# Scores of plain attentions: two tiles of 64 rows at a time, four neighbouring heads per tile, one spread of the keys for eight heads

## The chip, the core and the metric

One Trainium2 chip, one of its cores. The metric is the device time of one execution in microseconds; a smaller number is faster. The kernel before takes 2011.68 us, the median of 3 runs (2011.1 to 2012.37).

## What is computed

Four transformer layers, one after the other, on 16 sequences of 128 tokens with 256 features. Layer 0 has a small attention among the 16 heads of a token. Layer 1 has two attentions with quantised scores and weights. Layers 2 and 3 have two ordinary ("plain") attentions each, the ones that the change touches; all use 16 heads of 16 features. In the reference a plain attention is, cut to what matters (layer 2's form; layer 3 is the same with a mask of minus infinity in its second attention and none in its first):

```python
qh = split(q @ wq + bq)
kh = split(k @ wk + bk)
vh = split(v @ wv + bv)
logits = jnp.einsum('bhqd,bhkd->bhqk', qh, kh) / jnp.sqrt(jnp.float32(depth))
if mask is not None:
    logits = logits + mask * -1000000000.0
attn = jax.nn.softmax(logits, axis=-1)
out = jnp.einsum('bhqk,bhkd->bhqd', attn, vh)
```

Around each attention stand an output projection, a residual sum, a layer norm and, once per layer, a feed-forward net of width 1024. Everything is float32 here.

## The kernel before

The 16 sequences are worked in 4 groups; a group has two streams (`st` 0 and 1) of two sequences (G = 2). Each engine has its instructions written out in one fixed order. `together` lays the 13 steps of one stream's attention and the "pieces" of the other stream (projections, norm, transposes, feed-forward, the next keys) beside each other: on each engine step 0, its pieces, step 1, its pieces, and so on. On PE the pieces come after the step of their number; on ACT, DVE and POOL most come one step later (LATE = 1). Nothing is reordered at run time, so an instruction that waits holds all that stand behind it on its engine.

One attention of a stream has U = 8 units u: 2 sequences j times 4 sets of four heads. For a plain attention a unit goes through these stages:

- **Spread of the keys** (`spread`, line 1300, POOL). KT holds 128 rows, that is 8 heads of 16 rows. For unit u the tile KB gets four copies of the keys side by side, each with the rows of one head kept and all others zero (times own_head), so that one matmul gives the scores of four heads. Even units take heads 0, 2, 4, 6 of the eight, odd units 1, 3, 5, 7. There are 4 such tiles (NK), and the spreads run up to 3 units ahead (KEYS_AHEAD).
- **Scores** (`scores`, line 806, PE). One matmul over 128 rows and 512 columns into PSUM bank u % 2. It waits until the bank was read: by the mask addition of unit u - 2 where there is a mask, otherwise by the exponentials of unit u - 2. A float32 matmul stands in the trace as two instructions.
- **Mask and row maximum** (`shift`, lines 1183 and 1187, DVE). With a mask, line 1183 adds it and writes to the SBUF tile prob, which frees the bank; line 1187 takes the maxima.
- **Exponentials** (line 990, ACT), four per unit; from prob, or from the bank without a mask.
- **Turn** (`turn`, line 816, PE), four transposes, two steps later, and their copy to SBUF (line 976, ACT).
- **Values** (`values_pair`, line 850, PE) for two units together: products with V and with ones, in column tiles of 32. Then DVE divides (`outputs`, lines 1217 and 1219).

The quantised attentions of layer 1 already spread keys in bf16 for eight heads at once and use halves of 64 rows (lines 1295 and 804), one unit per step.

The plain attentions of layers 2 and 3 are 32: 4 groups, 2 layers, 2 streams, 2 attentions. In the order of time, the first attention of stream 0 and of stream 1 have the feed-forward's last product or its neighbours beside them, the second of stream 0 has the short pieces, the second of stream 1 has the next layer norm, projections and feed-forward.

## Time and profile before

| what | value |
|---|---|
| median of 3 runs | 2011.68 us |
| the profiled execution's own time | 2007.97 us |
| its span in the trace | 2006.2 us |
| PE busy | 1808.6 us (90%) |
| DVE busy | 1237.6 us (62%) |
| ACT busy | 1074.7 us (54%) |
| POOL busy | 905.3 us (45%) |

Times in the views count from the span's start. PE is the matmul engine, PEld its loading of weights, which lies beside the matmuls; DVE, ACT and POOL are VectorE, ScalarE and GpSimd. A matmul's duration in a row contains its latency, so matmuls that follow each other overlap in the rows; what one costs in a stream is the distance between starts. "Idle before" tells how long an engine stood still and what ended that. The chain of waits is followed back from the last instruction.

### The profile page before, as it was taken

The numbers are of one execution on the slowest core, as the hardware profiler recorded it, in microseconds if no ns is written. First come the engines' busy times: TensorE is split into PE (matmuls) and PEld (weight loads), VectorE is DVE, ScalarE is ACT, GpSimd is POOL, SyncE is SP. The second block draws the span as 40 slices with busy tenths as digits, with TensorE's granted clock in tenths as the row PEclk, the third lists the DMA queues.
The fourth block names the chain that finished last, engine by engine and source line by source line (L and its number), as shares of the span: only waits on it lengthen the run. The fifth ranks groups of instructions, "written<-read, shape, count | busy, mean of one in ns | idle before, by whom it ended". The sixth has DMA issues, their size and how long they took to land.

```text
span 2006.2 us, 34807 instructions
## 1 busy us (share of the span) xinstructions
PE 1808.6 (90%) x12481; PEld 1344.1 (67%) x12481; DVE 1237.6 (62%) x2220; ACT 1074.7 (54%) x3142; POOL 905.3 (45%) x1209
## 2 busy tenths in 40 slices
PE   4998988789799889889999999999999999999997
PEld 4887876466566656657667677676676676766766
DVE  5899995744654464463575665865746647365471
ACT  2232225665575475565575564655645656565662
POOL 4466554654463363363254443644444333333340
PEclk8999998788878878879999999999999999999999
DMA  7200000002000000000002000000000000000000
GB/s 226 92 11 6 11 6 6 1 7 90 1 6 6 1 6 6 0 6 7 1 7 90 1 7 6 7 7 1 7 6 2 12 1 7 22 7 1 12 1 11
DMA packets 31073, 35.66 MB, mean 18 GB/s; under 512 B 3164, under 2 KB 29752, under 8 KB 30520
## 3 DMA queue, kind: packets, MB, share of 16 engines
q1 hardware_dynamic: 30904, 33.44, 5.2%
q8 instruction: 102, 1.67, 0.3%
q14 instruction: 67, 0.55, 0.1%
HBM read 31.34 MB, written 2.10 MB: 17 GB/s over the span
## 4 chain that ended last, share of the span: by engine, by line
PE 61%; DVE 17%; ACT 10%; issue 6%; POOL 2%; SPq 2%; DMA 1%; DVEq 0%; POOLq 0%; ACTq 0%
PE ps L594 33%; PE ps L806 6%; PE ps L744 6%; PE ps L816 5%; PE ps L850 4%; ACT work L983 3%; ACT work L990 3%; DVE work L1183 3%; DVE xn L1037 2%; PE ps L607 2%; DVE rowmax L1187 2%; PE ps L831 2%; ACT hT L899 1%; PE ps L766 1%; POOL work L1376 1%
## 5 line engine op out<-in xcount | busy, mean ns | idle before, releaser
L594 PE MATMUL ps<-hT,w_slot 128*128 128x256 f32 x1696 | 410.1, 396 | 17.1 <-ACT hT L899 16.1
L1300 POOL TENSOR_TENSOR work<-KT,own_head 128x512 f32<-128x512 f32 x256 | 262.4, 1046 | 285.4 <-PE ps L806 179.9
L594 PEld LDWEIGHTS ps<-hT,w_slot 128*128 128x128 f32 x1696 | 323.5, 196 | 77.2 <-ACT hT L899 21.7
L990 ACT ACTIVATE work<-work,rowmax 128x128 f32<-128x128 f32 x768 | 244.9, 391 | 167.8 <-DVE rowmax L1187 167.0
L816 PEld LDWEIGHTS ps<-ident,work 128*128 128x128 f32 x1536 | 200.1, 153 | 170.0 <-issue 90.4
L983 ACT ACTIVATE work<-ps,rowmax,score_scale 128x128 f32<-128x128 f32 x512 | 229.3, 484 | 118.7 <-DVE rowmax L1191 118.3
L816 PE MATMUL ps<-ident,work 128*128 128x128 f32 x1536 | 266.4, 302 | 17.9 <-ACT work L990 17.0
L806 PE MATMUL ps<-work,QT 128*128 128x512 f32 x512 | 266.4, 605 | 10.0 <-POOL work L1300 4.9
L1376 POOL TENSOR_SCALAR work<-work,winv 128x128 f32<-128x128 f32 x512 | 185.0, 382 | 167.7 <-DVE winv L1203 165.3
L1217 DVE RECIPROCAL O<-ps 128x128 f32<-128x128 f32 x128 | 122.3, 955 | 174.6 <-PE ps L850 173.9
L976 ACT ACTIVATE work<-ps 128x512 f32<-128x512 f32 x256 | 150.7, 596 | 91.4 <-PE ps L816 91.2
L1316 POOL TENSOR_SCALAR vareps<-meanvar 128x2 f32<-128x2 f32 x88 | 19.3, 220 | 383.0 <-DVE meanvar L1030 379.9
L1059 DVE TENSOR_TENSOR x_all<-ps,x_all 128x512 f32<-128x512 f32 x72 | 49.7, 690 | 154.1 <-PE ps L594 89.0
L947 ACT ACTIVATE hid<-ps,vcols 128x256 f32<-128x256 f32 x192 | 80.7, 472 | 106.6 <-PE ps L594 106.5
L1037 DVE TENSOR_SCALAR xn<-x_all,meanvar,rstd 128x256 f32<-128x256 f32 x176 | 128.4, 769 | 13.0 <-POOL rstd L1318 12.7
L1187 DVE TENSOR_REDUCE rowmax<-work 128x4 f32<-128x512 f32 x192 | 131.8, 686 | 6.6
L1295 POOL TENSOR_TENSOR work<-QKb,own_quad 128x512 bf16<-128x512 bf16 x64 | 70.2, 1116 | 130.5 <-issue 125.0
L594 PE MATMUL ps<-w_slot,OT 128*128 128x256 f32 x448 | 119.6, 414 | 6.4 <-ACT OT L931 4.8
L804 PE MATMUL ps<-work,QKb 64*128 64x512 bf16 x128 | 62.8, 501 | 66.7 <-ACT work L983 47.7
L983 ACT ACTIVATION_READ_ACCUMULATOR work<-ps,rowmax,score_scale 128x1 f32 x512 | 118.2, 231 | 0.0
L744 PE MATMUL ps<-w_slot,hid 128*128 128x256 f32 x512 | 116.5, 381 | 1.6 <-ACT hid L947 0.9
L974 ACT ACTIVATE work<-ps,top 128x512 bf16<-128x512 f32 x128 | 90.5, 707 | 50.3 <-PE ps L816 49.3
(131 smaller groups left out, 3170.3 us busy)
## 6 DMA issues: line engine op xcount, KB each, us to landing
ctx_in<-in_ctx SPq DMA_DIRECT2D x32, 256.0 KB, 2.7
w_slot<-in_L_xattn_W SPq DMA_DIRECT2D x2, 1024.0 KB, 6.2
w_slot<-in_L_xattn_ff_w SPq DMA_DIRECT2D x1, 2048.0 KB, 11.5
w_slot<-in_L_xattn_ffn_w SPq DMA_DIRECT2D x2, 1024.0 KB, 9.8
w_slot<-in_L_xattn_w SPq DMA_DIRECT2D x2, 1024.0 KB, 10.0
out<-x_all SPq DMA_DIRECT2D x8, 256.0 KB, 2.1
x_all<-in_x SPq DMA_DIRECT2D x1, 1536.0 KB, 11.4
pad<-in_mask_Bx1x1xS_fk SPq DMA_DIRECT2D x1, 1024.0 KB, 7.6
```

Of the source, the lines that this page charges most:

```text
L594: mm = pe.matmul(dst, lhsT(k), rhs(k), start=(k == 0 and not onto), stop=(k == chunks - 1 and not more))
L744: mm = pe.matmul(one[:, j * D:(j + 1) * D], hid[:, k, tok(j)], w[arg["w2"]][:, k, :], start=(k == 0), stop=(k == FC - 1))
L806: pe.matmul(bank(u % 2), QT[st][:, m, tok(j)], KB[u % NK], start=True, stop=True).then_inc(s["scores_ps"], 1)
L816: mm = pe.transpose(bank(2 + u % 2)[:, tok(h)], prob[u % (NP if quant else NPF)][:, tok(h)], ident[:, :])
L976: act.activation(PTF[u % 4], bank(2 + u % 2), ACT.Copy).then_inc(s["PT_ready"], 1)
L983: ex = act.activation(prob[i % NP][:, tok(h)], bank(i % 2)[:, tok(h)], ACT.Exp, bias=shifts[:, at:at + 1], scale=score_scale[:, arg["quant ...
L990: ex = act.activation(prob[i % NPF][:, tok(h)], src[:, tok(h)], ACT.Exp, bias=shifts[:, at:at + 1])
L1037: dve.tensor_scalar(xn[st][:, j, :].unsqueeze(1), x_of(g, st, j), meanvar[st][:, j, 0:1], rstd[st][:, j:j + 1], ALU.subtract, ALU.mult).th ...
L1187: dve.tensor_reduce(shift_u, sc, AX.X, ALU.max, negate=True).then_inc(s["shift_ready"], 1)
L1217: dve.reciprocal(oinv[st][quarter], bank(4 + m)[:, sums_at:sums_at + S]).then_inc(s["oinv_ready"], 1)
L1300: pool.tensor_tensor(KB[u % NK].rearrange("p (h k) -> p h k", h=HU), keys, own_head[:, e:HC:2].unsqueeze(2).broadcast_to([P, HU, S]), ALU. ...
L1376: w = pool.tensor_scalar(prob[u % NP][:, tok(h)], prob[u % NP][:, tok(h)], winv[:, u // 2 % 2, at:at + 1], MAGIC, ALU.mult, ALU.add)
```

## The change

A plain attention now makes its scores for two units at once. At each even step PE issues the scores of units u and u + 1: rows 0 to 63 of QT and of one spread tile give the four lower heads into bank 0, rows 64 to 127 the four upper heads into bank 1. It is four matmuls of 64 rows and 256 columns: left half of the columns for both row halves, then right half. They signal once, by 2, at the end. The odd steps have no scores.

The wait ahead of them is for what has freed both banks: the mask addition of unit u - 1, or the exponentials of unit u - 1. The wait for V, which stood before the scores of unit 1, is now at step 1.

The spread is done once for two units, with the table own_four (row r belongs to head r // 16, folded to four columns), so 4 instead of 8 spreads per attention, of the same form. The 4 tiles hold the 8 units of an attention, and a spread waits only for the scores that used its tile in the attention before. The values take their columns from the turned tiles in the new order of heads; their number and form stay.

```diff
--- before.py
+++ after.py
@@ -276,6 +276,7 @@
         ident = sb("ident", [P, P])
         own_head = sb("own_head", [P, HC])
         own_quad = sb("own_quad", [P, HU], BF16)
+        own_four = sb("own_four", [P, HU])
         ones_pair = sb("ones_pair", [P, 4, DH])
         vcols = sb("vcols", [P, P])
         vcols_q = sb("vcols_q", [P, len(Q_BIASES) * C])
@@ -791,19 +792,24 @@
                         att = use("att", layer, g, n["att"])
                         pe.wait_ge(q["q_ready"], C * (att + 1))
                         pe.wait_ge(q["k_ready"], C * (att + 1))
-                    if u == 1:
-                        pe.wait_ge(q["v_ready"], G * (use("att", layer, g, n["att"]) + 1))
                     pe.wait_ge(s["KB_ready"], U * ap + u + 1)
-
-                    if u >= 2 and "mask" in arg:
-                        pe.wait_ge(s["masked"], U * masked_phase(layer, g, mix, st) + u - 1)
-                    else:
+                    if quant:
+
                         pe.wait_ge(s["exp_ready"], U * ap + u - 1)
-                    if quant:
                         half = slice(u % 2 * (P // 2), (u % 2 + 1) * (P // 2))
                         pe.matmul(bank(u % 2), QTb[st][half, m, tok(j)], KBb[u // 2][half, :], start=True, stop=True).then_inc(s["scores_ps"], 1)
+                        return
+
+                    if u and "mask" in arg:
+                        pe.wait_ge(s["masked"], U * masked_phase(layer, g, mix, st) + u)
                     else:
-                        pe.matmul(bank(u % 2), QT[st][:, m, tok(j)], KB[u % NK], start=True, stop=True).then_inc(s["scores_ps"], 1)
+                        pe.wait_ge(s["exp_ready"], U * ap + u)
+                    for part in range(2):
+                        cols = slice(part * US // 2, (part + 1) * US // 2)
+                        for e in range(2):
+                            half = slice(e * (P // 2), (e + 1) * (P // 2))
+                            mm = pe.matmul(bank(e)[:, cols], QT[st][half, m, tok(j)], KB[u // 2][half, cols], start=True, stop=True)
+                    mm.then_inc(s["scores_ps"], 2)
 
                 def turn(u):
                     if quant:
@@ -847,12 +853,14 @@
                         for e in range(2):
                             for h in range(HU):
                                 own = ones_pair[:, 2 * e:2 * e + 2, :] if summed else V[st][:, j, m * HU + h, 2 * e:2 * e + 2, :]
-                                mm = pe.matmul(bank(4 + m)[h * 32:(h + 1) * 32, cols], own, PTF[(u + e) % 4][:, tok(h)],
+                                mm = pe.matmul(bank(4 + m)[h * 32:(h + 1) * 32, cols], own, PTF[(u + h // 2) % 4][:, tok(2 * (h % 2) + e)],
                                                start=(e == 0), stop=(e == 1))
                     mm.then_inc(s["o_ps"], 2)
 
                 def step(i):
-                    if i < U:
+                    if i == 1:
+                        pe.wait_ge(q["v_ready"], G * (use("att", layer, g, n["att"]) + 1))
+                    if i < U and (quant or i % 2 == 0):
                         scores(i)
                     if 0 <= i - lag < U:
                         turn(i - lag)
@@ -1281,7 +1289,7 @@
                 q, mix, quant = c[st], n["att"], "quant" in arg
                 ap = phase("att", layer, g, mix, st)
 
-                j, m, e = u // UJ, u % UJ // 2, u % 2
+                j, m = u // UJ, u % UJ // 2
                 if u == 0 and layer == 1 and mix == 0 and st == 0 and g == 0:
 
                     pool.wait_ge(s["o_ready"], G * phase("mix", layer, g, mix, st))
@@ -1295,11 +1303,10 @@
                     pool.tensor_tensor(KBb[u // 2].rearrange("p (h k) -> p h k", h=HU), keys,
                                        own_quad[:, :].unsqueeze(2).broadcast_to([P, HU, S]), ALU.mult).then_inc(s["KB_ready"], 2)
                     return
-                pool.wait_ge(s["scores_ps"], U * ap + u + 1 - NK)
+                pool.wait_ge(s["scores_ps"], U * ap + u - 6)
                 keys = KT[st][:, m, tok(j)].unsqueeze(1).broadcast_to([P, HU, S])
-                pool.tensor_tensor(KB[u % NK].rearrange("p (h k) -> p h k", h=HU), keys,
-                                   own_head[:, e:HC:2].unsqueeze(2).broadcast_to([P, HU, S]), ALU.mult)\
-                    .then_inc(s["KB_ready"], 1)
+                pool.tensor_tensor(KB[u // 2].rearrange("p (h k) -> p h k", h=HU), keys,
+                                   own_four[:, :].unsqueeze(2).broadcast_to([P, HU, S]), ALU.mult).then_inc(s["KB_ready"], 2)
 
             def emit_piece(layer, g, st, ahead=False, shift={}):
                 q = c[st]
@@ -1308,7 +1315,7 @@
                 def emit(piece, arg, n):
                     if piece == "keys":
                         for u in range(KEYS_AHEAD):
-                            if "quant" not in arg or u % 2 == 0:
+                            if u % 2 == 0:
                                 spread(layer, g, st, arg, n, u)
                     elif piece == "norm":
                         k = due("norm", layer, g, n["norm"])
@@ -1380,7 +1387,7 @@
                 def step(i):
 
                     u = i + KEYS_AHEAD - 1
-                    if i > 0 and u < U and (not quant or u % 2 == 0):
+                    if i > 0 and u < U and u % 2 == 0:
                         spread(layer, g, st, arg, n, u)
                     if quant and 0 <= i - SUM_LAG - 1 < U:
                         weigh(i - SUM_LAG - 1)
@@ -1401,6 +1408,7 @@
                                pattern=[[DH, HC]], channel_multiplier=-1).then_inc(s["own_ready"], 1)
             pool.wait_ge(s["own_ready"], 1)
             pool.tensor_tensor(own_quad[:, :], own_head[:, 0:HU], own_head[:, HU:HC], ALU.add)
+            pool.tensor_tensor(own_four[:, :], own_head[:, 0:HU], own_head[:, HU:HC], ALU.add)
             pool.memset(neg_half[:, :], -0.5)
             pool.memset(top[:, :], MAGIC + 255.0)
             pool.memset(below[:, :], -255.0)
```

PE, from the third scores on, in the first attention of layer 3 (no mask), stream 1, as it was. `work,QT` are scores, `ident,work` the transposes of a unit, `work,V` and `work,ones_pair` the values of two units, `ident,xn` the other stream's transposes.

```order
L806 MATMUL ps<-work,QT 128x512
L816 MATMUL ps<-ident,work 128x128 x4
L806 MATMUL ps<-work,QT 128x512
L816 MATMUL ps<-ident,work 128x128 x4
L806 MATMUL ps<-work,QT 128x512
L816 MATMUL ps<-ident,work 128x128 x4
L850 MATMUL ps<-work,V 32x128 x8
L850 MATMUL ps<-work,ones_pair 32x128 x8
L806 MATMUL ps<-work,QT 128x512
L816 MATMUL ps<-ident,work 128x128 x4
L806 MATMUL ps<-work,QT 128x512
```

The same place on PE, from the second scores on, as it is now:

```order
L811 MATMUL ps<-work,QT 128x256 x4
L822 MATMUL ps<-ident,work 128x128 x8
L811 MATMUL ps<-work,QT 128x256 x4
L822 MATMUL ps<-ident,work 128x128 x4
L856 MATMUL ps<-work,V 32x128 x8
L856 MATMUL ps<-work,ones_pair 32x128 x8
L822 MATMUL ps<-ident,work 128x128 x4
L811 MATMUL ps<-work,QT 128x256 x4
L822 MATMUL ps<-ident,work 128x128 x4
L856 MATMUL ps<-work,V 32x128 x8
```

Before, a transpose of a finished unit stood between the scores of any two units. Now the second scores row carries units 4 and 5, and the transposes of unit 2 and all values of units 0 and 1 stand behind it.

POOL, between two attentions of layer 2: `KT,own_head` and `KT,own_four` are spreads, `vareps` and `rstd` the other stream's norm, the rest its x; as it was.

```order
L1300 TENSOR_TENSOR work<-KT,own_head 128x512 x6
L1316 TENSOR_SCALAR vareps<-meanvar 128x2
L1318 TENSOR_TENSOR rstd<-vareps,neg_half 128x2
L1300 TENSOR_TENSOR work<-KT,own_head 128x512 x2
L1325 TENSOR_TENSOR x_all<-xn,rows 128x512
L1328 TENSOR_TENSOR x_all<-x_all,rows 128x512
L1338 TENSOR_TENSOR x_all<-x_all,rows 128x512
```

The same place on POOL as it is now:

```order
L1308 TENSOR_TENSOR work<-KT,own_four 128x512 x3
L1323 TENSOR_SCALAR vareps<-meanvar 128x2
L1325 TENSOR_TENSOR rstd<-vareps,neg_half 128x2
L1308 TENSOR_TENSOR work<-KT,own_four 128x512
L1332 TENSOR_TENSOR x_all<-xn,rows 128x512
L1335 TENSOR_TENSOR x_all<-x_all,rows 128x512
L1345 TENSOR_TENSOR x_all<-x_all,rows 128x512
```

Three spreads in place of six lie together ahead of the norm, and one in place of two behind it.

## Rows read from the trace of the kernel before

**Rows 1.** The page, busy time of each engine (us, share of the span, instructions).

```profile
PE 1808.6 (90%) x12481; PEld 1344.1 (67%) x12481; DVE 1237.6 (62%) x2220; ACT 1074.7 (54%) x3142; POOL 905.3 (45%) x1209
```

**Rows 2.** The page, the chain that ended last, by engine and by line.

```profile
PE 61%; DVE 17%; ACT 10%; issue 6%; POOL 2%; SPq 2%; DMA 1%; DVEq 0%; POOLq 0%; ACTq 0%
PE ps L594 33%; PE ps L806 6%; PE ps L744 6%; PE ps L816 5%; PE ps L850 4%; ACT work L983 3%; ACT work L990 3%; DVE work L1183 3%; DVE xn L1037 2%; PE ps L607 2%; DVE rowmax L1187 2%; PE ps L831 2%; ACT hT L899 1%; PE ps L766 1%; POOL work L1376 1%
```

**Rows 3.** Windows; columns: length, busy PE, PEld, DVE, ACT, POOL, clock, DMA, GB/s.

```profile
1072.59:1111.98 39.39, 37.85 (x285) 28.95 (x284) 22.34 (x40) 21.34 (x58) 17.70 (x18) 1.00 0.34 114
1624.63:1655.89 31.26, 29.98 (x245) 21.95 (x244) 13.30 (x24) 17.55 (x49) 10.27 (x11) 1.00 0.00 1
1655.89:1681.71 25.82, 23.74 (x213) 15.69 (x212) 18.82 (x33) 16.46 (x46) 9.40 (x11) 1.00 0.01 2
950.00:1960.00 1010.00, 959.20 (x7815) 698.55 (x7814) 613.55 (x1100) 599.31 (x1642) 419.28 (x441) 1.00 0.03 10
```

**Rows 4.** Groups by line: busy us, mean ns of one; idle before, who ended it.

```profile
L806 PE MATMUL ps<-work,QT 128*128 128x512 f32 x512 | 266.4, 605 | 10.0 <-POOL work L1300 4.9 <-DVE V L1080 2.4 <-ACT work L990 2.3
...
L1300 POOL TENSOR_TENSOR work<-KT,own_head 128x512 f32<-128x512 f32 x256 | 262.4, 1046 | 285.4 <-PE ps L806 179.9 <-ACT KT L911 105.1
...
L804 PE MATMUL ps<-work,QKb 64*128 64x512 bf16 x128 | 62.8, 501 | 66.7 <-ACT work L983 47.7 <-DVE V L1011 10.9 <-DVE QKb L1011 5.8
...
L806 PEld LDWEIGHTS ps<-work,QT 128*128 128x128 f32 x512 | 85.6, 190 | 38.7 <-issue 20.8 <-DVE V L1080 10.6 <-POOL work L1300 2.0
```

**Rows 5.** Chain of waits, 1586.89 to 1716.68 us; start, us, what.

```profile
1651.39 1.73 PE ps L594 x8
```

**Rows 6.** Timeline of PE, masked attention that begins at 1072.59.

```profile
1072.59 1.02 PE L806 MATMUL ps<-work,QT 128*128 128x512 f32 x2
...
1077.24 1.02 PE L806 MATMUL ps<-work,QT 128*128 128x512 f32 x2
...
1094.00 1.02 PE L806 MATMUL ps<-work,QT 128*128 128x512 f32 x2
...
1097.19 1.99 PE L594 MATMUL ps<-w_slot,O 128*128 128x256 f32 x8 [0.73 <-ACT KT L911]
```

**Rows 7.** Timeline of DVE, same attention.

```profile
1093.71 0.68 DVE L1183 TENSOR_TENSOR work<-ps,look 128x512 f32<-128x512 f32 x1
```

**Rows 8.** Timeline of PE, unmasked attention that begins at 1624.63.

```profile
1638.65 1.10 PE L806 MATMUL ps<-work,QT 128*128 128x512 f32 x2 [0.57 <-ACT work L990]
...
1642.53 1.02 PE L806 MATMUL ps<-work,QT 128*128 128x512 f32 x2
1643.39 0.60 PE L816 MATMUL ps<-ident,work 128*128 128x128 f32 x4
1643.92 0.65 PE L850 MATMUL ps<-work,V 128*32 128x128 f32 x16
...
1645.42 1.02 PE L806 MATMUL ps<-work,QT 128*128 128x512 f32 x2
```

**Rows 9.** Timeline of DVE, same attention.

```profile
1641.26 0.96 DVE L1217 RECIPROCAL O<-ps 128x128 f32<-128x128 f32 x1 [0.79 <-PE ps L850]
```

**Rows 10.** Instructions of line 1037 (durations in ns, min/median/max).

```profile
L1037 DVE TENSOR_SCALAR xn<-x_all,meanvar,rstd x176: 395/412/4620, 58.7 to 1982.4; 128x256 f32<-128x256 f32 x176
```

**Rows 11.** Timeline of DVE around 1178 us.

```profile
1178.60 2.07 DVE L1037 TENSOR_SCALAR xn<-x_all,meanvar,rstd 128x256 f32<-128x256 f32 x2
```

**Rows 12.** Timeline of POOL, same stretch.

```profile
1178.19 1.28 POOL L1338 TENSOR_TENSOR x_all<-x_all,rows 128x512 f32<-128x512 f32 x1
1179.43 1.09 POOL L1300 TENSOR_TENSOR work<-KT,own_head 128x512 f32<-128x512 f32 x1
```

**Rows 13.** Timeline of PE in a quantised attention, 64-row score matmul and its successor.

```profile
312.36 0.39 PE L804 MATMUL ps<-work,QKb 64*128 64x512 bf16 x1 [0.74 <-DVE V L1011]
312.67 1.99 PE L594 MATMUL ps<-w_slot,OT 128*128 128x256 f32 x8
```

**Rows 14.** Windows in the same quantised attention (columns as in rows 3).

```profile
320.00:325.00 5.00, 4.46 (x22) 2.35 (x21) 4.08 (x13) 4.93 (x18) 4.74 (x12) 0.50 0.01 3
```

## The prediction

> **What bounds the kernel now.** I read the busy shares first: PE is busy for 90% of the span, DVE for 62%, ACT 54%, POOL 45% [rows 1]. The chain of waits says the same with less certainty: 61% of it is PE, 17% DVE, 10% ACT, and the plain score matmuls (line 806) are 6% of it, about 120 us [rows 2]. The windows then say where: the 32 plain attentions fill 950 to 1960 us, with PE busy for 959 of 1010 us and the granted clock at its upper level of 2.4 GHz throughout [rows 3]. That looks like a pure PE bound, and it is not quite one. In the masked attention without large pieces beside it (1655.89 to 1681.71) DVE is busy for 18.8 of 25.8 us, and a unit must pass score, mask, maximum, exponential, transpose, copy and values in turn. PE's order is fixed, so what counts is where PE's saving meets a wait. Layers 0 and 1, which end before that window, are untouched.
>
> **Part 1: the score matmuls themselves.** A float32 matmul of 256 columns costs 1.73 / 8 = 0.216 us per instruction, two instructions each [rows 5]. The score matmul of one unit has 512 columns and two instructions, so 4 x 0.216 = 0.86 us in a stream; this is also the distance from 1642.53 to 1643.39 [rows 8]. Two units: 1.73 us. The new block of four 64-row matmuls of 256 columns has eight instructions of 0.216 us. If the upper and lower rows run beside each other it takes 0.86 us, if not, 1.73 us. To this comes the change of shape of the array: full transposes started at 1643.39 and the column-tiled values at 1643.92, 0.53 us for four transposes that stream in 0.44, so 0.09 us for entering another tiling [rows 8]. For leaving the 64-row form, the bf16 score at 312.36 was followed 0.31 us later [rows 13], against 512 columns / 2.4 GHz = 0.21 us: 0.10 us. I take 0.86 + 0.09 + 0.10 and add 0.10 us for weights, since the block loads eight times where two units loaded four times: **1.15 us per block**, bounds 0.86 and 1.9 us. I stand near the lower end because the column-tiled values, also float32, do overlap: from 1643.92 to 1645.42 PE starts 32 of them and four transposes [rows 8], where 32 x 0.108 us one by one would be 3.5 us. PE's work shrinks by 128 x (1.73 - 1.15) = 74 us. The Trainium skill ("TensorEngine Tiling (Array Packing)", Key Properties) says that changing the tiling mode drains the engine; the 0.09 us agrees. The skill ("TensorE: Matmul & The Clock Gate", Measured speedup vs the span model) gives 3.07 for four row tiles; an estimate from that efficiency, 0.77, is a block of 1.12 us before the switches, and by it the gain below would be about 7 us smaller.
>
> **Part 2: the coarser wait.** Before, the scores of u waited for the bank of u - 2. Now the block of u and u + 1 waits for u - 1, and the transposes of u - 2 and the values of u - 4 and u - 3 are queued behind it. DVE and ACT wait for these. I went through the eight kinds of attention with PE's new order and the old durations; two show the pattern.
> *Masked, with the feed-forward beside it (from 1072.59).* Three score matmuls, of units 1, 3 and 5, go ahead of the one at 1094.00 [rows 6], 2.6 us. But the last block needs the mask addition of unit 5, which began at 1093.71 and took 0.68 us [rows 7]. DVE is early only by the one matmul (0.86) that stood before its first block. So the block starts at 1093.71 + 0.68 + 0.15 - 0.86 = 1093.7 and some 2 us of the saving become waiting. The next piece waited for KT, which ACT writes behind the exponentials of unit 5 (1097.19 [rows 6]); it comes about 1 us sooner, and with the score of unit 7 gone from behind it the attention ends 1.4 us sooner.
> *Unmasked, stream 1 (from 1624.63).* Block (4, 5) waits for the exponentials of unit 3, some 0.75 us later than the old wait for unit 2 at 1638.65 [rows 8]. Then come: block and transposes 1.3, values 1.1, the reciprocal (0.96 [rows 9]) and its product 0.3, the norm 0.7, the maximum 0.7, the exponentials of unit 5 1.2: block (6, 7) starts 6.3 us after block (4, 5), at 1645.7, where unit 6 started at 1642.53 and unit 7 at 1645.42. The transposes and values that used to stand between 6 and 7 now come after. This one ends **2.1 us later** even with a perfect block.
> With a block of 0.86 us, layer 2 gains 1.4, 1.0, 0.6 and 0.9 us in its four attentions per group, and layer 3 gains 0.3, -2.1, 0.25 and 0.4. Four groups: 4 x (3.9 - 1.15) = **11 us gained**. With 1.15 us instead, the excess of 0.3 us shows once or twice per attention, mostly in the tail where PE is never idle: 8 kinds x 0.45 x 4 = 14, say **15 us lost**.
>
> **Part 3: POOL.** 256 spreads of 1.05 us become 128, so 134 us less [rows 4]. POOL is at 45%, and its spreads mostly stood waiting for the scores (179.9 us of idle before them), so by itself this is worth nothing; no POOL wait becomes longer, since a spread now needs only scores of the attention before. But DVE's normalisation (line 1037) takes 0.41 us at the median and up to 4.6 [rows 10]; at 1178.60 two of them took 2.07 us [rows 11], while POOL ran x and then a spread from 1179.43 [rows 12]. It seems to be held by the POOL instruction that runs. One of the two spreads behind the norm disappears. I count 0.7 us in each kind with a spread between, 0.4 to 0.5 in the others, none in one: 3.9 us per group, and all of it is ahead of the block (6, 7): 4 x 3.9 = **16 us gained**, bounds 0 and 20.
>
> **Sum.** 11 - 15 + 16 = 12 us. The profiled execution took 2007.97 us (span 2006.2), so 1996; against the median of 2011.68, which is 3.7 us above it, **2000 us**. With the block at 0.86 us it is 1985, and without the POOL term 2016. About 4 us (0.2%) is what a measurement can tell from no change.
>
> **The rivals.**
> *A, the halves don't overlap (0.13).* The trace has no float32 row tiles side by side. The weights of a score matmul load in 190 ns [rows 4]; two such loads lie in one pass of 216 ns only if loads overlap as well. The skill ("TensorE: Matmul & The Clock Gate", LDWEIGHTS) says that a load's time goes with columns, not rows, which is against this change. A block of 1.9 us, 0.75 more than taken, costs 4 x 8 x 0.45 / 0.3 x 0.75 = 36 us: 2036. It decides from a block of about 1.4 us on.
> *B, slower by the coarser wait (0.17).* If DVE and ACT have less slack than I read, each masked attention loses its 1 us gain and 0.5 more, at the last block: 24 x 1.5 = 36 us worse than the sum, 2036; with half of it, 2018. For it speaks the DVE-bound stretch of 1655.89 [rows 3]; against it that most blocks there are issued while DVE does other pieces.
> *C, much faster (0.15).* The chain gives line 806 6% of the span [rows 2]; if PE truly bounds, 74 us less work shortens the span by some 45: 1967. Against it: the waits in part 2.
> *D, the clock falls (0.06).* In the quantised attentions PE did little for some microseconds and the clock granted was 0.50, that is 1.2 GHz [rows 14]. The plain attentions now give PE longer waits. If 1.5 us of PE work in each of 16 short attentions takes twice as long, that is 24 us: 2024.
> *E, nothing to see (0.10).* Parts 2 and 3 cancel: 2012.
>
> **How the numbers follow.** The forecast, 1985 to 2006, has 0.39. Faster by over 0.2%: 0.39 + C 0.15 = 0.54. Within 0.2%: most of E and a little of B, 0.13. Slower: A, D, the rest of B and E, 0.33. The range leaves out what lies beyond C and A: 1967 to 2036.
>
> **What would show it.** Right: the distance from a block's start to the next instruction is 1.1 to 1.2 us; PE idles before line 811 for exponentials or masked tiles, in all by tens of us; PE busy falls by 60 to 80 us while the span falls by 12; the first unmasked attention of stream 1 is 2 to 3 us longer and those of layer 2 are 1 us shorter; two normalisations take 0.8 to 1.4 us instead of 2. Wrong: a distance of 1.7 us or more (A), the masked attentions of layer 2 longer (B), all eight kinds 1.5 us shorter (C), a granted clock below 1.00 between 950 and 1960 us (D).

## The result, and the profile after

The changed kernel takes 2027.86 us (median of 4 runs, 2026.9 to 2029.31) beside 2011.39 us of the kernel before: ratio 1.0089, 95% interval 1.0075 to 1.0103. It is slower by 0.9%, where 2000 us was forecast. The value lies in the range, the sign is wrong. The profiled execution took 2029.31 us with a span of 2027.6 us.

The page's busy times and its groups on the lines that changed (line 806 is now 811, line 1300 is 1308; columns as in [rows 1] and [rows 4]):

```profile
PE 1761.1 (87%) x12993; PEld 1359.9 (67%) x12993; DVE 1211.4 (60%) x2220; ACT 1078.7 (53%) x3142; POOL 774.8 (38%) x1082
...
L811 PE MATMUL ps<-work,QT 64*128 64x256 f32 x1024 | 150.3, 411 | 75.0 <-DVE work L1191 37.3
L1308 POOL TENSOR_TENSOR work<-KT,own_four 128x512 f32<-128x512 f32 x128 | 130.6, 1041 | 126.5 <-issue 126.5
```

PE works 48 us less and POOL 131 us less, as meant. But PE's idle time ahead of the score matmuls went from 10.0 us [rows 4] to 75.0. Another view of line 811 lists what ended it:

```profile
  DVE work L1191: 37.3, 46
  ACT work L998: 33.1, 12
```

The mask addition ended 37.3 us of it, in 46 waits of less than 1 us on average; the exponentials ended 33.1 us in only twelve waits. Both are the new wait for the unit just before.

**The block.** The timeline of PE in the masked attention that begins at 1073.61 us, the one of [rows 6]:

```profile
1079.95 3.62 PE L745 MATMUL ps<-w_slot,hid 128*128 128x256 f32 x16
1083.50 1.14 PE L811 MATMUL ps<-work,QT 64*128 64x256 f32 x8
1084.57 1.09 PE L822 MATMUL ps<-ident,work 128*128 128x128 f32 x8
...
1094.14 1.14 PE L811 MATMUL ps<-work,QT 64*128 64x256 f32 x8 [0.30 <-DVE work L1191]
```

From 1079.95 to the block are 3.55 us for 16 instructions that stream in 16 x 0.216 = 3.46, so entering costs 0.09 us; from the block's start to the next instruction are 1.07 us. Together 1.16 us, where 1.15 was taken. The single starts in the trace show the rest: the two matmuls of a pair (upper and lower rows) start 7 ns apart, the second pair 0.32 us behind the first, the third and fourth 0.216 us each, and the transposes 0.31 us behind the last pair. So the two row halves run side by side completely, and 0.10 us behind the first pair and 0.09 us for leaving come on top.

**The unmasked attention of stream 1**, the kind of [rows 8], as PE's timeline shows it:

```profile
1503.70 1.14 PE L811 MATMUL ps<-work,QT 64*128 64x256 f32 x8 [2.96 <-ACT work L998]
1504.76 0.66 PE L822 MATMUL ps<-ident,work 128*128 128x128 f32 x4
1505.35 0.65 PE L856 MATMUL ps<-work,V 128*32 128x128 f32 x16
...
1510.34 2.08 PE L811 MATMUL ps<-work,QT 64*128 64x256 f32 x8 [3.33 <-ACT work L998]
1512.36 1.11 PE L822 MATMUL ps<-ident,work 128*128 128x128 f32 x4
1513.40 1.08 PE L856 MATMUL ps<-work,V 128*32 128x128 f32 x16
```

and the windows of the changed kernel (columns as in [rows 3]): this attention whole, its stretch from the first block to the second wait's end and the stretch behind that, the 1010 us of the plain attentions, and the masked short attention of layer 3 twice, in two groups.

```profile
1488.68:1525.99 37.31, 30.30 (x262) 23.68 (x261) 14.74 (x30) 16.34 (x48) 9.64 (x11) 0.91 0.01 1
1503.70:1510.34 6.64, 3.32 (x48) 2.41 (x49) 3.83 (x8) 3.34 (x10) 2.14 (x3) 0.93 0.01 4
1510.34:1517.20 6.86, 6.86 (x56) 5.08 (x56) 2.46 (x4) 2.44 (x7) 3.25 (x3) 0.57 0.00 0
...
950.00:1960.00 1010.00, 892.57 (x8161) 700.16 (x8161) 574.29 (x1073) 592.15 (x1611) 287.40 (x312) 0.98 0.03 10
...
1525.99:1551.49 25.50, 21.20 (x229) 15.82 (x228) 18.38 (x33) 16.66 (x46) 5.23 (x6) 1.00 0.01 2
1663.47:1690.08 26.61, 22.49 (x230) 16.90 (x229) 18.39 (x33) 16.73 (x46) 5.24 (x6) 0.94 0.01 2
```

PE stood idle for 2.96 us, then for 3.33 us, and behind the second wait its clock was at 1.2 GHz for most of 6.9 us: the block took 2.02 us instead of 1.06, the transposes 1.04 instead of 0.59. In this execution the clock fell in all four unmasked attentions of stream 1, in three of the four of stream 0 (39.7 us each, 38.2 where it held), in one of the four short masked attentions of layer 3 (the last two rows show the same instructions with a clock of 1.00 and of 0.94, 1.1 us apart) and in the last attention of all. From 950 to 1980 us it stood at 1.2 GHz for 48 us; work at half the clock takes twice as long, so that costs at most 24 us. In [rows 3] the clock was 1.00 throughout. The Trainium skill ("TensorE: Matmul & The Clock Gate", HAM oscillation — how this bites in real kernels) describes a kernel in which every wait for a DMA throttles the work behind it anew. The trace agrees in part: the waits here are for ScalarE, and behind the first one, of 2.96 us, the work still ran at full clock; only behind the second it was slow.

**The normalisation.** The pair of [rows 11], 2.07 us there:

```profile
1177.40 1.03 DVE L1045 TENSOR_SCALAR xn<-x_all,meanvar,rstd 128x256 f32<-128x256 f32 x2
```

### The profile page after: what moved, and what is told of

Its sections match the earlier page's. It is cut to its first block, busy times and chain, and to the rows that moved or that the text cites. A ratio compares the mean times of both kernels' runs of the same rounds, so it can differ in the third digit from the quotient of the medians.

```text
span 2027.6 us, 35704 instructions
## 1 busy us (share of the span) xinstructions
PE 1761.1 (87%) x12993; PEld 1359.9 (67%) x12993; DVE 1211.4 (60%) x2220; ACT 1078.7 (53%) x3142; POOL 774.8 (38%) x1082
## 4 chain that ended last, share of the span: by engine, by line
PE 58%; DVE 19%; ACT 10%; issue 7%; POOL 2%; SPq 2%; DMA 1%; DVEq 0%; POOLq 0%; ACTq 0%
PE ps L595 32%; PE ps L745 6%; PE ps L822 5%; PE ps L856 5%; PE ps L811 4%; DVE work L1191 4%; ACT work L991 3%; ACT work L998 3%; PE ps L608 2%; DVE xn L1045 2%; DVE rowmax L1195 2%; PE ps L767 2%; PE ps L837 2%; DVE O L1225 2%; ACT hT L907 2%
## 5 line engine op out<-in xcount | busy, mean ns | idle before, releaser
L822 PE MATMUL ps<-ident,work 128*128 128x128 f32 x1536 | 275.8, 311 | 20.3 <-ACT work L998 19.8
L822 PEld LDWEIGHTS ps<-ident,work 128*128 128x128 f32 x1536 | 194.6, 156 | 108.1 <-issue 53.1
L811 PE MATMUL ps<-work,QT 64*128 64x256 f32 x1024 | 150.3, 411 | 75.0 <-DVE work L1191 37.3
L1308 POOL TENSOR_TENSOR work<-KT,own_four 128x512 f32<-128x512 f32 x128 | 130.6, 1041 | 126.5 <-issue 126.5
L811 PEld LDWEIGHTS ps<-work,QT 64*128 64x128 f32 x1024 | 96.0, 191 | 114.0 <-issue 110.9
```

Of the source, the lines that this page charges most:

```text
L811: mm = pe.matmul(bank(e)[:, cols], QT[st][half, m, tok(j)], KB[u // 2][half, cols], start=True, stop=True)
L822: mm = pe.transpose(bank(2 + u % 2)[:, tok(h)], prob[u % (NP if quant else NPF)][:, tok(h)], ident[:, :])
L1308: pool.tensor_tensor(KB[u // 2].rearrange("p (h k) -> p h k", h=HU), keys, own_four[:, :].unsqueeze(2).broadcast_to([P, HU, S]), ALU.mult) ...
```

## The experiments

The theory after reading this trace: the wait for the unit just before costs more than the overlap of the halves gives, above all in the unmasked attentions, and the slow clock is part of the price. It left open whether the halved spreads gave anything: behind that pair of normalisations the mask addition then waited 1.53 us for PE.

**1 and 2. Where the loss is.** Each kernel has the new block, wait and spread only in the attentions with a mask (24 of the 32), or only in the 8 without, and the form of before in the others. Because the two forms share the four tiles, a spread of the new form waits here for up to three more scores of the attention before (`u // 2 - 3` in place of `u - 6`; the same in kernels 11 and 12). In the first kernel the attentions of layer 2 take as long as in the changed one (37.9, 31.1 or 31.6, and 23.6 us for the first three kinds), so that costs nothing that can be seen.

```diff
+ if not ("mask" in arg):    # 2: if not ("mask" not in arg)
+     the wait, score matmul and spread of the kernel before, unit by unit
```

> The change is made in the 24 masked attentions only; the 8 without a mask (layer 3, first) keep the old scores, waits and eight spreads. Theory W (the loss sits in the unmasked attentions: their exponentials free the banks late, PE waits about 3 us twice per attention and its clock then falls to 1.2 GHz): all the gains and none of the loss are left, about 2011 - 15 = 1996 us, granted clock 1.00 from 950 to 1940 us. Rival S (the loss is spread over all attentions: tiling switches and the coarser wait anywhere): three quarters of the 16 us stay, about 2023 us.

> The change is made in the 8 unmasked attentions only. Theory W: they alone lose about 32 us (4 x 2 and 4 x 6), so about 2043 us, slower than the change as a whole, and the clock falls in them. Rival S: a quarter of the loss, about 2015 us.

Measured: 1999.34 us for the masked ones alone (1995.27 to 2001.32), ratio 0.9948 [0.9933, 0.9962], and 2034.2 us for the unmasked ones alone, 1.0122 [1.0108, 1.0136]. The score rows of the two kernels:

```profile
L818 PE MATMUL ps<-work,QT 64*128 64x256 f32 x768 | 111.8, 409 | 37.4 <-DVE work L1198 37.4
L808 PE MATMUL ps<-work,QT 128*128 128x512 f32 x128 | 67.0, 605 | 7.0 <-POOL work L1316 4.7 <-ACT work L1005 2.3
```

```profile
L808 PE MATMUL ps<-work,QT 128*128 128x512 f32 x384 | 199.4, 605 | 2.7 <-DVE V L1095 2.4
L818 PE MATMUL ps<-work,QT 64*128 64x256 f32 x256 | 39.8, 430 | 37.3 <-ACT work L1005 32.7 <-POOL work L1320 4.6
```

The two effects, -0.5% and +1.2%, come to 0.7% together, near the 0.9% of the whole change. In the 24 masked attentions the new form gains 10 us, 0.4 each, although PE waits 37.4 us for the mask; in the 8 unmasked ones it loses 24 us, 3 each. Both times are nearer to theory W's 1996 and 2043 us than to rival S's 2023 and 2015. One thing of theory W did not come: in the first kernel the clock between 950 and 1960 us was 0.99 and not 1.00, since it fell in three of the four short masked attentions of layer 3. Rival B put the danger in the masked ones, the wrong place.

In the second kernel the clock held in one of the four unmasked attentions of stream 1 and fell in the other three. Two of the four, with the same matmuls:

```profile
1498.16:1532.67 34.51, 27.51 (x262) 22.05 (x262) 14.75 (x30) 16.22 (x48) 10.62 (x12) 1.00 0.01 2
1631.49:1668.44 36.95, 30.41 (x262) 23.76 (x262) 13.10 (x24) 17.61 (x49) 7.18 (x8) 0.91 0.00 1
```

Of the 5.7 us that such an attention takes longer than the 31.26 of [rows 3], the waits are 3.3 and the clock 2.4.

**3. What the clock costs.** In the unmasked attentions of the changed kernel, five matmuls whose result is not used (256 columns, into a free bank) ahead of block (4, 5), and in stream 1 ahead of block (6, 7) too.

```diff
+ if "mask" not in arg and (u == 4 or (u == 6 and st == 1)):
+     pe.wait_ge(s["PT_ready"], U * ap + u - 3)
+     for _ in range(5):
+         pe.matmul(bank(2)[:, 0:T], ident[:, :], QT[st][:, m, :], start=True, stop=True)
```

> The change with five extra matmuls of 256 columns (2.2 us of PE work, the result is overwritten unused) ahead of the block of units 4 and 5 in each unmasked attention, and of units 6 and 7 in stream 1, where PE waits for exponentials for about 3 us. Nothing else is done sooner. If the fallen clock is the larger part of the loss (theory W with clock): the clock stays at 1.00, the unmasked attention of stream 1 takes 34 instead of 37.3 us, and the whole 2028 - 18 = 2010 us. If the wait itself is all of it (theory W without clock): 2028 us or some us more.

Measured 2012.64 us (11 runs, 2011.4 to 2016.06), ratio 1.0016 [1.0007, 1.0025]. Its timeline of PE, same place:

```profile
1502.79 2.32 PE L806 MATMUL ps<-QT,ident 128*128 128x256 f32 x10
1506.19 1.13 PE L815 MATMUL ps<-work,QT 64*128 64x256 f32 x8 [1.08 <-ACT work L1002]
1507.26 0.65 PE L826 MATMUL ps<-ident,work 128*128 128x128 f32 x4
```

Work that nobody needs took 15 us off. The attention took 34.4 us, as expected, at a clock of 1.00. The block still waits for the exponentials and starts 21.5 us behind the attention's start, 21.7 without them; only what stands behind it runs at 2.4 GHz. In this kernel the clock fell in all four short masked attentions of layer 3 instead of in one.

**4. The fall there too.** Four more such matmuls ahead of block (6, 7) in those four attentions.

```diff
+ if layer == 3 and "mask" in arg and u == 6 and st == 0:
+     the same wait, and four of the same matmuls
```

> The warm kernel (the changed kernel with matmuls whose result is not used, ahead of late blocks in the unmasked attentions; 2012.6 us) with four more of them, 1.7 us, ahead of block (6, 7) in each of the four masked attentions of stream 0 in layer 3. In the warm kernel the clock still fell in these four, and the attention took 26.66 us where the changed kernel without a fall took 25.51 us. If the fall is what costs there: 2012.6 - 4 x 1.1 = 2008 us, and the clock's whole part of the changed kernel is some 20 us. If the added matmuls only fill a wait that the mask sets anyway and the clock falls elsewhere: 2012 to 2014 us.

Measured 2009.83 us (12 runs, 2007.66 to 2014.68), ratio 1.0005 [0.9996, 1.0013]. The granted clock is back at 1.00 between 950 and 1960 us (first row; the other two are the four groups of layer 2 and the first three of layer 3). The short attentions took 25.8 us in three groups and 26.09 in one, where 25.51 were measured without added matmuls and without a fall: the matmuls cost 0.3 us there themselves.

```profile
950.00:1960.00 1010.00, 921.15 (x8464) 722.82 (x8463) 589.05 (x1099) 600.55 (x1639) 290.52 (x316) 1.00 0.03 10
...
942.39:1445.98 503.59, 453.42 (x4225) 357.22 (x4225) 324.47 (x593) 305.02 (x834) 169.51 (x178) 1.00 0.04 14
1445.98:1843.06 397.08, 366.72 (x3283) 286.81 (x3283) 209.03 (x402) 231.49 (x628) 97.13 (x113) 1.00 0.02 7
```

So the slow clock costs 1.0089 - 1.0005, 0.84% or **17 us** (14 to 20 by the intervals): the whole of the loss against before, not the whole of the miss. The traces agree, 1015.1 us from the first to the last plain attention's start in the changed kernel and 999.1 here. The added matmuls' own cost hides in this difference, so it is rather a little too small. The step from kernel 3 to 4 alone, 2 us by the ratios, is not clear of the noise.

**5. The spreads alone.** The kernel before, with one spread for two units.

```diff
- pe.matmul(bank(u % 2), QT[st][:, m, tok(j)], KB[u % NK], start=True, stop=True)
+ pe.matmul(bank(u % 2), QT[st][:, m, tok(j)], KB[u // 2], start=True, stop=True)
- pool.wait_ge(s["scores_ps"], U * ap + u + 1 - NK)
+ pool.wait_ge(s["scores_ps"], U * ap + u - 6)      # and only for even u
```

> The kernel before with one spread for two units and nothing else changed; both units multiply the full 128 rows with it, so each of their scores sums over two heads (that part of the result is left wrong, the work of TensorE, VectorE and ScalarE is as before). If the third term of the prediction is right (the spreads hold VectorE's normalisation, 16 us of it on the path), it takes 1995 us. If the freed time of VectorE and POOL ends in a wait of TensorE or of the exp instead, it takes 2008 to 2012 us.

In the code that ran, the spread keeps the table of before and its even heads, so the odd unit repeats the even unit's scores and the odd heads are left out. Other than the expectation says, no score sums over two heads. The same holds for kernel 8. The work is the same either way.

Measured 1996.96 us (1994.23 to 2001.28), ratio 0.9934 [0.9922, 0.9947]: 13 us (11 to 16) gained. By the traces the gain sits in four of the eight kinds of attention: 0.7 and 0.5 us in the first two of layer 2, 0.5 and 1.1 in the last two of layer 3, nothing in the other four.

This also tells what kernel 1 gained. Its 1999.34 us are no better than these 1996.96, and all of the spreads' gain lies in masked attentions. So the masked attentions gain by GpSimd's halved work; beside kernel 5 the new scores bring them 0.6 to 2.0 us per group in layer 2 and cost them 0.3 us per group in layer 3, 1.4 where the clock falls.

**6. The spreads doubled in the changed kernel**, the second copy into a spare tile.

```diff
+ pool.tensor_tensor(spare, keys, own_four, ALU.mult)    # waits for the spare's last write
  pool.tensor_tensor(KB[u // 2], keys, own_four, ALU.mult)
```

> The changed kernel, but GpSimd writes each spread a second time into a spare tile, so that its work in the plain attentions is again that of the kernel before. If the halved spreads save 16 us in the changed kernel, it takes 2044 us; if they save nothing there, because the block's wait ends on the exp of the unit before and not on VectorE, 2027 to 2031 us.

Measured 2046.32 us (2043.94 to 2051.21), ratio 1.0178 [1.0164, 1.0192], 18 us more than the changed kernel. Some of it is clock and not spreads: the clock fell in all four short masked attentions of layer 3 (one in the changed kernel), and from 950 us on it stood low for 14 us more, which costs 3 us at least (three short attentions at 1.1 us) and 7 at most. What is left, 11 to 15 us, agrees with kernel 5. The normalisation's group in the kernels before, 5, after and 6 (busy us, mean ns of one):

```profile
L1037 DVE TENSOR_SCALAR xn<-x_all,meanvar,rstd 128x256 f32<-128x256 f32 x176 | 128.4, 769 | 13.0 <-POOL rstd L1318 12.7
```

```profile
L1037 DVE TENSOR_SCALAR xn<-x_all,meanvar,rstd 128x256 f32<-128x256 f32 x176 | 107.1, 649 | 13.5 <-POOL rstd L1317 13.4
```

```profile
L1045 DVE TENSOR_SCALAR xn<-x_all,meanvar,rstd 128x256 f32<-128x256 f32 x176 | 105.4, 640 | 12.4 <-POOL rstd L1325 12.3
```

```profile
L1045 DVE TENSOR_SCALAR xn<-x_all,meanvar,rstd 128x256 f32<-128x256 f32 x176 | 125.1, 751 | 13.3 <-POOL rstd L1331 13.2
```

The third term of the prediction stands: the group follows the number of spreads, by some 20 us, and more than half of it reaches the end. In kernel 5 VectorE is busy 21.8 us less than before, 21.3 of it in this group. My doubt from the one place at 1177.40 us was wrong. The Trainium skill ("SBUF — State Buffer", SBUF: two separate sides) describes VectorE and GpSimd holding a shared pair of ports by turns, for a whole instruction; these four rows agree with it. They don't show that it is the ports.

**7. The coupling alone.** The kernel before, with both full-row scores of a pair at the even step, behind the coarse wait.

```diff
- if i < U:
-     scores(i)
+ if i < U and i % 2 == 0:    # behind the wait for unit i - 1
+     scores(i)
+     scores(i + 1)
```

> The kernel before with its full-row matmuls and its eight spreads, but both scores of a pair stand at the even step, behind the wait for the exp (or mask) of the unit just before: the coupling alone, without its gain. The changed kernel lost 16.5 us against 74 us less PE work and some 15 us of slow clock, so the coupling should cost about 75 us if the spreads gave nothing (2087 us), about 91 us if they gave 16 us (2103 us). If coupling costs little where TensorE has full-row work to do (it covers the waits), and the 64-row blocks themselves are what is slow, it takes under 2050 us.

Measured 2078.44 us (2074.85 to 2078.59), ratio 1.0331 [1.0316, 1.0345]: 67 us lost. Since the spreads do give 13 us or so, the expectation that counts is 2103, and it was 25 us too high. What is more, the 91 us in it were meant without slow clock, and these 67 are not: the unmasked attentions of stream 1 take 36.9 us here where the clock held and 39.5 to 42.8 where it fell, the short masked ones 26.4 and 28.0 to 28.1, together some 17 us. So the order alone costs full-row scores about 50 us. The expectation had taken it that all 74 us of saved PE work reach the end; kernel 8 shows that they don't.

**8. All but the overlap.** Kernel 7 with both parts of the diff of kernel 5.

> The changed kernel's order, waits and halved spreads, but each block is two full-row score matmuls of 512 columns (1.7 us and more instead of 1.06; each score then sums over two heads, so that part of the result is left wrong). Its distance to the changed kernel (2027.9 us) is what the overlap of the row halves really brings to the end in this order. If TensorE bounds the attentions, all of the 0.67 us in 128 blocks shows: 2027.9 + 86 = 2114 us. If the halved spreads save the same 14 to 18 us here as in the two kernels in which they were varied alone, it is the coarse kernel (2078.4 us) less that: 2060 to 2064 us, and only some 34 us of the 86 reach the end, the rest being time in which TensorE would wait for the mask or the exp in any case.

The runs fall into two bundles, 2058.5 to 2059.2 us (three) and 2074.0 to 2076.1 us (three; median of all 2066.57, ratio 1.029 [1.0258, 1.0322]). Between 31 and 48 us lie between it and the changed kernel. The expectation's 86 us was too high, since it left the 0.09 us for entering out; by 1.73 - 1.16 us it is 73. So 31 to 48 of 73 us, about half of the PE work that the overlap saves, reach the end. The profile is of the lower bundle. The upper one was not profiled; its mean clock over the execution is 0.919 to 0.923, that of the lower 0.930, so the slow clock is the likely difference. The score rows of kernels 7 and 8:

```profile
L808 PE MATMUL ps<-work,QT 128*128 128x512 f32 x512 | 259.1, 630 | 69.5 <-ACT work L997 33.4 <-DVE work L1190 31.4 <-POOL work L1307 4.6
```

```profile
L808 PE MATMUL ps<-work,QT 128*128 128x512 f32 x512 | 253.9, 619 | 62.3 <-ACT work L997 33.5 <-DVE work L1190 24.1 <-POOL work L1307 4.6
```

With 73 us more PE work in them these two idle ahead of the scores nearly as long as the changed kernel, 69.5 and 62.3 us against 75.0: the waits come from the order, not from the scores being faster.

**9. The order inside a step.** In the unmasked attentions the transpose and the values of a step stand ahead of the block, not behind it.

```diff
+ if not quant and "mask" not in arg:
+     turn(i - lag); values_pair(i - lag - 2)    # each under its own condition
+     if i % 2 == 0: scores(i)
+     return
```

> The change with PE's order inside an even step of an unmasked attention turned round: transposes of unit u - 2 and the values of the pair before it come ahead of the block of u and u + 1 instead of behind it. Theory W: the waits ahead of the block are filled with 1.5 us of work that ACT and DVE need, block (6, 7) comes about 1 us sooner with 1.5 us less behind it, the clock holds: stream 1 about 31 us, the whole 1995 to 2000 us. If only the exponentials' chain counts (not what is queued behind the block), it gains little: 2020 to 2028 us.

Measured 2000.65 us (1996.43 to 2003.13), ratio 0.9953 [0.9939, 0.9967]. PE's timeline in the unmasked attention of stream 1 that begins at 1484.27 us:

```profile
1499.31 1.14 PE L811 MATMUL ps<-work,QT 64*128 64x256 f32 x8
1500.38 0.66 PE L822 MATMUL ps<-ident,work 128*128 128x128 f32 x4
1502.40 0.66 PE L822 MATMUL ps<-ident,work 128*128 128x128 f32 x4 [1.37 <-ACT work L1006]
...
1504.93 1.13 PE L811 MATMUL ps<-work,QT 64*128 64x256 f32 x8 [0.86 <-ACT work L1006]
```

The waits of 2.96 and 3.33 us have become several of at most 1.4 us, the clock stays up here, and the attention takes 33.2 us instead of 37.3 (31 were expected). Where the clock held, it took 34.4 in kernel 4 and 34.5 in kernel 2, so covering the waits brings 1.2 us here and the clock most of the rest; in stream 0 it is 36.5 us against 38.2 with the clock up.

**10. The same in the masked attentions.**

```diff
- if not quant and "mask" not in arg:
+ if not quant:
```

> The changed kernel with the turn and the values ahead of the block in the masked attentions too. TensorE idles 2.0 to 3.6 us in each masked attention of the changed kernel, most of it ahead of blocks that wait for the mask. If that wait can be covered by the turn and the values, as it was without a mask, it takes 1985 to 1993 us. If the chain scores, exp, mask, sum is what sets the masked attentions' length, later scores lengthen it: 2002 to 2015 us.

Measured 2075.82 us (2074.39 to 2078.78), ratio 1.0327 [1.0312, 1.0341]: 75 us worse than kernel 9, far outside both expectations. The transposes' group of the changed kernel, then of kernel 10:

```profile
L822 PE MATMUL ps<-ident,work 128*128 128x128 f32 x1536 | 275.8, 311 | 20.3 <-ACT work L998 19.8 <-POOL work L1383 0.5
```

```profile
L822 PE MATMUL ps<-ident,work 128*128 128x128 f32 x1536 | 278.0, 310 | 118.5 <-ACT work L1006 117.9
```

PE now waits 118.5 us for exponentials, with a block behind it in the queue; the blocks themselves find their wait over when their turn comes (8.0 us of idle time ahead of line 811, where the changed kernel has 75.0). A masked block needs the mask addition, which comes before the exponential; the turn needs the exponential. Putting the turn first makes the scores wait for the longer half of the chain. The clock suffers too, 0.97 between 950 and 1960 us; how much of the 75 us that is was not measured.

**11 and 12. Built from the results.** Blocks in the masked attentions as in the change; in the unmasked ones of stream 0 the turns first; in those of stream 1, where even that order took 33.2 us against 31.3 [rows 3], the form of before. Kernel 12 adds the four unused matmuls of experiment 4.

```diff
- block, wait and spread of before: if not ("mask" in arg)
+ block, wait and spread of before: if not ("mask" in arg or st == 0)
+ turns first: if not quant and "mask" not in arg and st == 0
```

> The changed kernel's blocks in the masked attentions, its blocks with turn and values ahead of them in the unmasked attentions of stream 0, and the kernel before's form in the unmasked attentions of stream 1. With the blocks in the masked attentions alone it took 1999.3 us, and a stream-0 unmasked attention took 37.74 us there against 36.50 us with the turn ahead of the block. If the four gains of 1.24 us add up: 1994 us. If the time that stream 0 saves becomes waiting in stream 1: 1998 to 2001 us.

> The mixed kernel (1993.1 us) with the same four unused matmuls ahead of block (6, 7) in the masked attentions of stream 0 in layer 3. Its trace shows a clock fall in two of these four. If each costs 1.1 us: 1991 us, just at what a measurement can tell. If the matmuls come in the way of the block: 1993 to 1997 us.

Measured 1993.12 us (1991.39 to 1994.04), ratio 0.9912 [0.99, 0.9924], and 1990.03 us (1987.41 to 1990.81), ratio 0.9898 [0.9884, 0.9913]. Both beat the kernel before, by 0.9% and 1.0%. Whether kernel 12 is faster than 11 is open: all four of its runs are below the five of kernel 11, but the two intervals overlap. In the traces the clock falls in two short masked attentions of kernel 11 (26.6 us, 25.5 in the other two) and in none of kernel 12 (25.8 in all four), 1 us less in all.

## Why the prediction was wrong

**Part 1, the block: right.** 1.16 us measured, 1.15 taken. Rival A is out. The rule on weights that was set against the change (a load's time goes with columns) holds in the trace, with a median of 187 ns for a 64-row load, and did little harm: the pairs of matmuls still follow each other by 0.216 us, and only the first pair is 0.10 us longer, as much as was taken for weights.

**Part 3, POOL: right in kind, near in size.** 13 us in kernel 5, and 11 to 15 of kernel 6's 18, where 16 was taken from one place and counts. The gain came in four kinds of attention (2.9 us per group) and not, as counted, in seven (3.9), so that the size is near partly by luck.

**Part 2, the coarser wait: right in kind and place, the cost taken too small.** In the unmasked attention of stream 1, block (6, 7) was put at 1645.7 us, 21.1 us behind the start; it came after 21.7. In the masked one the last block was put at 1093.7 us and came 20.5 us behind its start, at 1093.1 by the clock of before. What the parts 1 and 2 give together is seen between kernel 5 (no block, half the spreads) and kernel 4 (blocks, clock up): ratios 0.9934 and 1.0005, a loss of 14 us, where 11 - 15 made a loss of 4. By the rows of kernel 4 above and those of kernel 5 here (first layer 2 whole, then three groups of layer 3), layer 2 gained 4.9 us where the prediction has 4 x (3.9 - 1.9) = 8, and layer 3 lost 13.0 / 3 = 4.3 us per group where it has 1.15 + 1.9 = 3.1; of that 0.3 us are the added matmuls'. Together 8 us too well priced by the traces and 10 by the ratios, spread over several attentions.

```profile
941.29:1449.74 508.45, 486.44 (x3969) 358.39 (x3968) 324.94 (x593) 304.67 (x834) 169.70 (x178) 1.00 0.04 14
1449.74:1833.84 384.10, 368.13 (x2977) 268.33 (x2977) 211.40 (x402) 230.25 (x628) 97.30 (x113) 1.00 0.03 7
```

**The step that failed: the sum has no term for the clock.** It was priced as rival D (0.06), with 24 us in 16 short attentions, and the 17 us came in seven of the 8 unmasked ones, one short masked one and the last. The size was near, the place and the chance were wrong. The prediction itself puts block (6, 7) 6.3 us behind block (4, 5), and names 1.3 and 1.1 us of PE's work in between, so that PE has to wait for nearly 4 us there (the window of 6.64 us above has it busy for 3.32). This was read as lateness only, though [rows 14] showed that the clock does fall in an attention of this kernel. For its cause those rows are no evidence: rival D says that PE did little there, but the window has PE busy for 4.46 of 5 us at 0.50; what went before isn't in it.

The balance in ratios: spreads -0.7%, blocks with the coarser wait +0.7%, clock +0.8%, together the measured 0.9%, or 18 us. From the 12 us of gain in the sum to this loss are 30 us: 17 of clock, 10 in parts 1 and 2, 3 in the spreads. The three were measured one behind the other, each as a difference of two kernels, so they add up by their making; each is good to about 3 us.

Of the signs named ahead: the distance of 1.1 us, the idle time ahead of line 811 and the shorter pair of normalisations came as foreseen, and the attentions of layer 2 got shorter, by 0.3 to 1.5 us (37.9 us for the 39.39 of [rows 3]); PE busy fell by 48 us and not by 60 to 80 (behind the second wait above, PE was busy for all of 6.86 us at a clock of 0.57, so slow clock counts as busy time), the attention of stream 1 grew by 6 us and not by 2 to 3, and the clock fell below 1.00, the sign for rival D.

## What to carry to other kernels

When a step is merged with its neighbour, list each wait that grows, and ask of each what TensorE has queued behind it: here two waits of some 3 us in a row were paid a second time through the clock. Which order covers it depends on what releases the wait: work that needs the exponential may stand ahead of a block that needs the exponential too, and must not stand ahead of one that needs only the mask. A change that loses as a whole can be worth keeping in parts: the masked attentions alone gained 0.5%, the mixture 0.9%. Ask then what the part earns: the halved spreads alone, without the new scores, gave 0.7% (kernel 5, which leaves out the odd heads), so most of the gain comes from GpSimd's smaller work and not from TensorE's. Not tried was the obvious middle way, blocks of 64 rows whose two halves each wait for their own bank only.

## What was not expected of the hardware

- Matmuls whose result nobody reads made the kernel faster, by 15 us for 60 of them (kernel 3) and perhaps 2 us more for 16 (kernel 4).
- The same instructions with the same waits (0.28, 0.21, 0.73 and 2.16 us) ran once with the clock at 1.00 and once at 0.94, 1.1 us apart (25.50 and 26.61 us above). Waits alone don't tell whether it falls.
- Halving a helper's instructions on GpSimd took 0.12 us off each of VectorE's 176 normalisations on average, 0.77 to 0.65 us.
- The upper and lower 64 rows of the array ran float32 matmuls side by side without loss: the two of a pair start 7 ns apart, and a block takes 1.07 us, entering not counted, for what takes 1.73 us in full rows.
